# One transformer layer on one core: the first norm's rows loaded a second time by quadrants and turned by VectorE

## The chip, the cores and the metric

The kernel runs on one core of a Trainium2 chip. A core has TensorE (matrix products and the transposes that it makes as products with an identity, results in PSUM), VectorE, ScalarE and GpSimd (elementwise work; GpSimd cannot reach PSUM), SyncE, whose queue SP issues all DMA transfers here, and 16 DMA engines. The engines run their own lists of instructions and meet at semaphores. The metric is the time of one execution on the device in microseconds (us). Lower is better.

## The reference

Input is x, 2 x 2048 rows of 1024, f32. "Attention" is taken over the 32 heads of one row, not over rows:

```python
h = layernorm(x)                                   # (x - mean) / sqrt(var + 1e-5)
q, k, v = (h @ w.T + b for w, b in ...)            # each [row, 32 heads, 32]
scores = einsum('bshd,bstd->bsht', q, k) / sqrt(32)
x = x + einsum('bsht,bstd->bshd', softmax(scores), v)
h = layernorm(x)
gates = h @ gate_w.T                               # 8 experts, top 2, softmax over the two
x = x + h @ base_w.T + base_b + 2.0 * sum_e w_e * (h @ lora_A[e].T) @ lora_B[e].T
```

## The kernel before

**Tiles.** The 4096 rows are 32 tiles of 128 rows, one tile per step t. All weights stay in SBUF as f16 pairs, a high and a low part, and each f32 product is made of two or three f16 products. Step t makes tile t's projections (k, q, v; each in two halves of 512 columns, `project`, L1164 and L1173), its scores and its softmax, and for tile p = t - 1 the context product, the second norm, the experts and the base projection (`dense`, L1274). Steps 0, 1 and 31 are written out, steps 2 to 30 are a hardware loop on each compute engine; SP's list is unrolled. Step 0 and the first part of step 1 also prepare the weights (scales, splits into parts), so engines work there in another order.

**TensorE's order in a step:** k half 0, context of t - 1, k half 1, q half 0, q half 1, `turn2` (the second norm's transposes of tile t - 1), v half 0, v half 1, `experts`, attention scores (`attend`, L1227), then `dense_all`: 24 products for half 0, 6 for half 1, `turn1(t + 1)`, 9 more, `turn_low`, 9 more, `dense_lora`. `turn1` and `turn2` are eight f32 transposes of 128x128 each through `turn_rows` (L1235), into the PSUM tile `attn_ps` (called `rows_ps` in this layout).

**The first norm of tile t + 1**, done during step t:

- SP loads the rows into `ld` (L432, 128 pieces of 4 KB), once `centred` says that the tile before has left it.
- ScalarE, `centre`: sum of the row (L608), negated mean (L610), `xn = ld - mean` (L612), sum of squares (L614). It stands behind `x2_high` and ahead of b's high part (L686).
- GpSimd, `row_root`: three operations on one column (L478, L480, L482), rstd.
- ScalarE, `row1_scale`: `xn *= rstd` (L619).
- TensorE, `turn1`: transposes of `xn`.
- ScalarE, `x1_high` (L583), and VectorE, `x1_low` (L903): the transposed rows as f16 high and low parts, `x_hi` and `x_lo`, which the next step's projections read.

`xn` is used by the second norm as well (`norm2`, L847, by VectorE; then `turn2`, `x2_high` L591, `x2_low` L908).

**The rest of the chain to the scores of tile t.** VectorE adds the biases to k (L891), turns each row's heads (`turn_first`, L989); ScalarE takes k's high part (L677, semaphore `a_hi_ready`), VectorE its low part (`first_low`, L994); SP spreads both to a block diagonal (`spread_k`, L404, eight transfers). VectorE adds q's biases, makes `x2_low`, turns q (L1089); ScalarE takes q's high part (L686), GpSimd its low part (`second_lo`, L492, semaphore `b_lo_ready`). `attend` waits for `b_lo_ready` and for the spread k. VectorE then adds v's biases (two L891), and turns v when q's low part is made (L1097). After the scores follow the softmax (L1105, L1107, ScalarE's exp L698, L1113 to L1117), its transpose (L1123) and spreading of v's parts by ScalarE and VectorE (L342) for the context product.

**Semaphores.** Engines work their lists in order. A wait stops everything behind it on that engine.

Of the kernel before, what the change touches and what calls it, by code (L numbers as in the profile page):

```python
# [27 lines left out]
P = 128  # L28
QD = 32
NQ = P // QD  # L30
# [34 lines left out]
def block_kernel(nc, x, wT, agT, lora_b, biases, out):  # L65
    T = x.shape[0] // P
    with ExitStack() as ctx:
# [40 lines left out]
        rstd1 = columns[:, 16:17]  # L108
# [11 lines left out]
        w_chunk_sum = sb("w_chunk_sum", [P, NG, KC])  # L120
# [43 lines left out]
        xn = carve(HID)  # L164
        ev = carve(HID)
# [32 lines left out]
        squares = sb("squares", [P, HID], F16)  # L198
# [67 lines left out]
        centred = sem("centred")  # L266
# [4 lines left out]
        row1_ready = sem("row1_ready")  # L271
# [76 lines left out]
        flag_ps = low_ps[:, P:2 * P]  # L348

# [16 lines left out]
        def _(sp):  # L366
# [55 lines left out]
            def step(t, prev, nxt):  # L422
                if prev:

                    sp.wait_ge(x1_ready, t)
                    sp.dma_start(res, rows(x, t)).then_inc(res_loaded, 16)
                first_hi(t)
                first_lo(t)
                if t + 2 < T:

                    sp.wait_ge(centred, t + 1)
                    sp.dma_start(ld, rows(x, t + 2)).then_inc(ld_loaded, 16)  # L432
                if t == 1:

                    sp.wait_ge(w_lo_done["base"], KC)
                    sp.dma_start(lora_up[:, :], lora_b).then_inc(lora_loaded, 16)
                if prev and nxt:

                    sp.wait_ge(base_free, 2 * t + 2)
                    sp.dma_start(rows(out, t - 1), y).then_inc(y_stored, 16)  # L440
                elif not prev:

                    sp.wait_ge(w_lo_done["v"], KC)
                    sp.dma_start(res, rows(x, 0)).then_inc(res_loaded, 16)
# [18 lines left out]
        def _(pool):  # L463
# [11 lines left out]
            def row_root(t):  # L475
# [6 lines left out]
                nc.gpsimd.tensor_tensor(rstd1[:, :], root1[:, :], x_scale[:, :], ALU.mult).then_inc(rstd_ready1, 1)  # L482
# [30 lines left out]
            def step(t, prev, nxt):  # L513
                if prev:
                    root(t - 1, var_ready2, rstd_ready2)
                    base_bias(t - 1, x1)
                if nxt:
                    row_root(t + 1)
                if prev:
                    second_lo(t)  # L520
                v_low(t)
# [8 lines left out]
        def _(act):  # L530
# [49 lines left out]
            def x1_high(t):  # L580

                act.wait_ge(turned1, t + 1)
                nc.scalar.copy(x_hi[:, :, :], rows_ps).then_inc(xhi_ready, 1)  # L583
# [15 lines left out]
            def centre(t, prev):  # L599

                act.wait_ge(ld_loaded, 16 * (t + 1))
                if prev:

                    act.wait_ge(turned2, t - 1)
                else:

                    act.wait_ge(turned1, 1)
# [4 lines left out]
                nc.scalar.activation(xn, ld, ACT.Identity, bias=neg_mean[:, 0:1]).then_inc(centred, 1)  # L612
                act.wait_ge(centred, t)
                nc.scalar.activation(squares[:, :], xn, ACT.Square, accum_out=square_sum[:, :]).then_inc(squared, 1)  # L614

            def row1_scale(t):

                act.wait_ge(rstd_ready1, t)
                nc.scalar.activation(xn, xn, ACT.Copy, scale=rstd1[:, 0:1]).then_inc(row1_ready, 1)  # L619
# [11 lines left out]
            def first_step():  # L631
# [9 lines left out]
                centre(1, False)  # L641
                gate_sums()
                row1_scale(1)
# [6 lines left out]
                sums("base", 3, 5)  # L650

# [17 lines left out]
            def step(t, prev, nxt):  # L669
                if not prev:  # L670
                    return first_step()

# [6 lines left out]
                if nxt:  # L679
                    centre(t + 1, prev)  # L680
# [6 lines left out]
                if nxt:  # L687
                    row1_scale(t + 1)
# [36 lines left out]
        def _(dve):  # L725
# [173 lines left out]

            def x1_low(t):  # L900

                dve.wait_ge(xhi_ready, t + 1)
                nc.vector.tensor_tensor(x_lo[:, :, :], rows_ps, x_hi[:, :, :], ALU.subtract).then_inc(xlo_ready, 1)  # L903
# [7 lines left out]
            dve.wait_ge(consts_set, EXPERTS + 4)  # L911
# [69 lines left out]
            def norm2(p, rows_before, x1):  # L981

                dve.wait_ge(turned1, rows_before)
# [13 lines left out]
            def first_step():  # L997
# [43 lines left out]
                scale("ag")  # L1041
                x1_low(1)
# [26 lines left out]
            def step(t, prev, nxt):  # L1069
                if not prev:  # L1070
                    return first_step()
                if prev:
# [5 lines left out]
                    norm2(t - 1, t + 1, x1)  # L1078
# [13 lines left out]
                add_bias(t, 0, "v", 1, v_acc, v_biased)  # L1092
                add_bias(t, 1, "v", 2, v_acc, v_biased)
# [44 lines left out]
            def tail(t):  # L1138
# [3 lines left out]
                norm2(t - 1, t, x1_last)  # L1142
# [12 lines left out]
        def _(pe):  # L1155
# [41 lines left out]
            def spread_max(g):  # L1197

                pe.wait_ge(max_diags, SCALED.index(g) + 1)
                nc.tensor.matmul(late_max_ps if g in ("ag", "base") else max_ps, ones[:, :], max_diag, start=True,  # L1200
# [37 lines left out]
            def turn1(t):  # L1238

                pe.wait_ge(row1_ready, t)  # L1240
                pe.wait_ge(shifted, t)
                turn_rows(turned1)
# [57 lines left out]
            def dense_all(p):  # L1300
# [19 lines left out]
            def first_step():  # L1320
# [28 lines left out]
                turn1(1)  # L1349
# [4 lines left out]
            def step(t, prev, nxt):  # L1354
# [16 lines left out]
                project(SECOND, 0, 2, b_acc, any_low[0])  # L1371

# [72 lines left out]
```

## Time and profile before

| | |
|---|---|
| median of 3 runs (lowest, highest) | 1361.64 us (1360.42, 1361.67) |
| the profiled execution: time, span | 1360.58 us, 1358.4 us |
| mean granted TensorE clock | 0.987 |
| busy: TensorE, its weight loads | 1297.6 us (96%), 688.9 us (51%) |
| busy: VectorE, ScalarE, GpSimd | 1077.9 us (79%), 689.0 us (51%), 259.8 us (19%) |
| DMA | 33047 packets, 87.41 MB, 64 GB/s |

All durations come from the profiled execution. Its time is 2.2 us longer than its span, which goes from the first to the last instruction. A line of the profile names kernel line, engine, operation, tiles (`work` is one buffer that holds ld, xn, res, x1, y, turned and others; `columns` holds single columns such as mean and rstd) and count, and in brackets how long the engine had been idle before and what released it. PE is TensorE, PEld its weight loads, DVE VectorE, ACT ScalarE, POOL GpSimd.

### The profile page before, as it was taken

How to read it: one execution, taken by the hardware profiler on the slowest of the kernel's cores; microseconds unless marked ns; L12 is line 12 of the kernel's file. 1: busy time of each engine (PE TensorE's matmuls, PEld its weight loads, DVE VectorE, ACT ScalarE, POOL GpSimd, SP SyncE). 2: the span in 40 equal slices, each digit the busy share in tenths (PEclk: the TensorE clock that was granted, in tenths of full speed). 3: DMA queues.
4: the chain of work that ended last, by engine and by line, in shares of the span. 5: the costliest groups of instructions: out<-in, count | busy, mean ns of one | idle time of the engine just before them, and what ended most of it. 6: DMA issues, size and time to landing. Idle time of an engine off the chain costs nothing.

```text
span 1358.4 us, 29896 instructions
## 1 busy us (share of the span) xinstructions
PE 1297.6 (96%) x12446; PEld 688.9 (51%) x12446; DVE 1077.9 (79%) x1556; ACT 689.0 (51%) x987; POOL 259.8 (19%) x239
## 2 busy tenths in 40 slices
PE   4767999999999999999999999999999999999996
PEld 1443555555555555555555555555555555555553
DVE  5878887887788778877887887788778877887874
ACT  6774445544454555445445544454555445445531
POOL 0011121222112122221121222112122221121220
PEclk9988999999999999999999999999999999999998
DMA  9521111111111111111111112111111111111110
GB/s 368 206 78 38 64 57 46 46 62 62 62 49 45 60 46 46 62 62 62 41 52 46 46 62 62 62 50 45 59 47 47 62 62 62 40 52 46 31 48 31
DMA packets 33047, 87.41 MB, mean 64 GB/s; under 512 B 6656, under 2 KB 7680, under 8 KB 33024
## 3 DMA queue, kind: packets, MB, share of 16 engines
q1 hardware_dynamic: 33024, 87.10, 19.5%
q8 instruction: 15, 0.25, 0.1%
q14 instruction: 8, 0.07, 0.0%
HBM read 53.52 MB, written 16.78 MB: 52 GB/s over the span
## 4 chain that ended last, share of the span: by engine, by line
PE 89%; DVE 4%; ACT 3%; issue 2%; DMA 0%; SPq 0%; POOL 0%; DVEq 0%; ACTq 0%; POOLq 0%
PE acc L1164 23%; PE dense_acc L1274 23%; PE acc L1173 23%; PE attn_ps L1227 7%; PE attn_ps L1235 4%; PE dense_acc L1282 4%; PE low_ps L1257 1%; PE low_ps L1259 1%; PE low_ps L1258 1%; ACT work L342 1%; PE dense_acc L1297 1%; ACT base_parts L540 1%; DVE base_parts L798 1%; DVE v_parts L798 1%; ACT w_hi_q L564 0%
## 5 line engine op out<-in xcount | busy, mean ns | idle before, releaser
L1274 PE MATMUL dense_acc<-base_parts,x 128*128 128x512 f16 x1488 | 334.7, 379 | 0.0
L342 ACT COPY work<-work 32x512 f16<-32x512 f16 x384 | 236.0, 614 | 8.8
L1274 PEld LDWEIGHTS dense_acc<-base_parts,x 128*128 128x128 f16 x1488 | 143.1, 98 | 160.3
L891 DVE SCALAR_TENSOR_TENSOR work<-acc,acc_to_a,biases_sb 128x512 f32<-128x512 f32 x192 | 143.7, 750 | 83.4 <-PE acc L1173 77.8
L677 ACT CAST work<-work 128x1024 f16<-128x1024 f32 x31 | 32.4, 1046 | 338.6 <-DVE work L989 338.6
L487 POOL TENSOR_TENSOR columns<-columns 128x1 f32<-128x1 f32 x33 | 18.1, 549 | 647.1 <-DVE columns L841 647.1
L1164 PE MATMUL acc<-w_hi_q,x_hi 128*128 128x512 f16 x496 | 118.9, 383 | 5.9 <-DVE work L891 5.9
L1164 PE MATMUL acc<-w_hi_k,x_hi 128*128 128x512 f16 x496 | 120.5, 387 | 2.4 <-issue 2.4
L1173 PE MATMUL acc<-w_hi_q,x_lo 128*128 128x512 f16 x496 | 118.4, 382 | 0.0
L1173 PE MATMUL acc<-w_hi_k,x_lo 128*128 128x512 f16 x496 | 117.2, 379 | 0.0
L1164 PE MATMUL acc<-v_parts,x_hi 128*128 128x512 f16 x496 | 117.2, 379 | 0.0
L1173 PE MATMUL acc<-v_parts,x_lo 128*128 128x512 f16 x496 | 117.2, 379 | 0.0
L1227 PE MATMUL attn_ps<-work 128*32 128x128 f16 x6144 | 97.8, 220 | 8.7 <-ACT work L342 6.2
L1227 PEld LDWEIGHTS attn_ps<-work 128*32 128x32 f16 x6144 | 86.6, 97 | 26.0 <-issue 14.8
L498 POOL TENSOR_TENSOR work<-work 128x1024 f16<-128x1024 f32 x32 | 68.1, 2127 | 114.7 <-ACT work L693 109.4
L693 ACT CAST work<-work 128x1024 f16<-128x1024 f32 x31 | 32.4, 1045 | 104.0 <-DVE work L1097 104.0
L1164 PEld LDWEIGHTS acc<-w_hi_q,x_hi 128*128 128x128 f16 x496 | 48.8, 99 | 65.6 <-DVE work L891 6.4
L504 POOL TENSOR_TENSOR work<-work,biases_sb 128x1024 f32<-128x1024 f32 x32 | 75.6, 2362 | 32.0 <-DVE work L847 32.0
L1164 PEld LDWEIGHTS acc<-w_hi_k,x_hi 128*128 128x128 f16 x496 | 46.7, 99 | 68.9 <-issue 23.2
L968 DVE STREAM_TRANSPOSE work<-attn_ps 128x1024 f32<-128x1024 f32 x32 | 62.2, 1944 | 22.6 <-PE attn_ps L1227 22.6
L1235 PE MATMUL attn_ps<-ident,work 128*128 128x128 f32 x512 | 68.2, 277 | 11.8 <-DVE work L847 11.8
L1173 PEld LDWEIGHTS acc<-w_hi_q,x_lo 128*128 128x128 f16 x496 | 48.9, 99 | 59.7 <-issue 2.2
(184 smaller groups left out, 2065.1 us busy)
## 6 DMA issues: line engine op xcount, KB each, us to landing
work<-x_dram SPq DMA_DIRECT2D x64, 512.0 KB, 3.5
work<-work SPq DMA_DIRECT2D x256, 64.0 KB, 2.0
out_dram<-work SPq DMA_DIRECT2D x31, 512.0 KB, 2.9
work<-wT_dram SPq DMA_DIRECT2D x17, 512.0 KB, 5.6
v_parts<-wT_dram SPq DMA_DIRECT2D x8, 512.0 KB, 13.8
base_parts<-wT_dram SPq DMA_DIRECT2D x5, 512.0 KB, 10.8
biases_sb<-bias_dram SPq DMA_DIRECT2D x4, 512.0 KB, 7.5
base_parts<-agT_dram SPq DMA_DIRECT2D x1, 544.0 KB, 9.7
```

The source lines that it names most:

```text
L342: copy(diag[c * QD:(c + 1) * QD, :, c, j::NQ, :], src).then_inc(vdiag_ready, 1)
L498: nc.gpsimd.tensor_tensor(v_parts_t[:, :, 1, :], turned3, v_parts_t[:, :, 0, :], ALU.subtract).then_inc(v_lo_ready, 1)
L504: nc.gpsimd.tensor_tensor(x1, x1, bias["base"][:, :], ALU.add).then_inc(x1_biased, 1)
L677: nc.scalar.copy(k_parts[:, 0, :, :], turned3).then_inc(a_hi_ready, 1)
L891: nc.vector.scalar_tensor_tensor(out=ev[:, s], in0=acc[bank][:, :], scalar=acc_to_a[:, i:i + 1], in1=bias[g][:, s], op0=ALU.mult, op1=ALU. ...
L968: nc.vector.transpose(turned.rearrange("p (h d) -> p d h", h=HEADS), attn_ps[:, :].rearrange("p (t d) -> p d t", t=QD)).then_inc(ctx_turne ...
L1164: nc.tensor.matmul(dst, x_hi[:, k, :], w_hi[g][:, k, cols], start=(k == 0), stop=False)
L1173: mm = nc.tensor.matmul(dst, x_lo[:, k, :], w_hi[g][:, k, cols], start=False, stop=(k == KC - 1))
L1227: mm = nc.tensor.matmul(attn_ps[c * QD:(c + 1) * QD, i4 * P:(i4 + 1) * P], dense_parts[:, i, dense_part, :], diag[:, spread_part, :, i, :] ...
L1235: mm = nc.tensor.transpose(rows_ps[:, k, :], xn[:, k * P:(k + 1) * P], ident[:, :])
L1274: nc.tensor.matmul(dense_acc[n][:, :], rows_part[:, k, :], w_part[:, k, cols], start=(k == 0 and m == 0), stop=False)
L1282: nc.tensor.matmul(dense_acc[n][:, :], low[:, :], lora_up[:, n * HALF:(n + 1) * HALF], start=False, stop=True).then_inc(base_acc, 1)
```

## The change

The first norm of tiles 1 to 31 no longer passes through TensorE's transposes. (Tile 0 stays as it was.) VectorE's transpose turns each 32x32 block of a tile in place. So the rows are loaded a second time, in an order in which block-wise turning gives the whole transpose: partition 32b + t of the new layout holds, for each of 8 chunks k and 4 quadrants q, 32 elements of row 32q + t. Each piece of that load is 32 elements, 128 bytes, 1024 pieces for each of four transfers. Since a partition now holds four different rows, it needs their four means and rstds. They are carried by a product: `same_row` (128x128, one where two partitions have the same number within their quadrant) times `stat_rows` (each row's rstd and -mean * rstd, placed in the columns of its own quadrant).

```diff
 # SP
+            def load_quads(t):
+                sp.wait_ge(squared, t)
+                src = rows(x, t).rearrange("(q t) (k b c) -> b t k q c", q=NQ, b=NQ, c=QD)
+                for b in range(NQ):
+                    dst = ld[b * QD:(b + 1) * QD, :].rearrange("t (k q c) -> t k q c", k=KC, q=NQ)
+                    sp.dma_start(dst, src[b]).then_inc(quads_loaded, 16)
...
             def step(t, prev, nxt):
                 if prev:
+                    if nxt:
+                        load_quads(t + 1)
                     sp.wait_ge(x1_ready, t)
                     sp.dma_start(res, rows(x, t)).then_inc(res_loaded, 16)
                 first_hi(t)
                 first_lo(t)
+                if not prev:
+                    load_quads(1)
+                    sp.wait_ge(w_lo_done["v"], KC)
+                    sp.dma_start(res, rows(x, 0)).then_inc(res_loaded, 16)
                 if t + 2 < T:
-                    sp.wait_ge(centred, t + 1)
+                    sp.wait_ge(x1_turned_ready, t + 1)
                     sp.dma_start(ld, rows(x, t + 2)).then_inc(ld_loaded, 16)
 # GpSimd, row_root: behind rstd1; row_root(t + 1) now stands ahead of root(t - 1)
+                nc.gpsimd.tensor_tensor(neg_mean_rstd, rstd1, neg_mean[:, :], ALU.mult).then_inc(shift_ready1, 1)
+                pool.wait_ge(shift_ready1, t)
+                nc.gpsimd.tensor_tensor(stat_rows[:, :, :], row_stats[:, :].unsqueeze(2).to_broadcast([P, 2, NQ]),
+                                        in_quad[:, :].unsqueeze(1).to_broadcast([P, 2, NQ]),
+                                        ALU.mult).then_inc(stat_rows_ready, 1)
 # ScalarE
-            def centre(t, prev):  ...   # sum, mean, xn = ld - mean, sum of squares
-            def row1_scale(t):    ...   # xn *= rstd
+            def row_statistics(t):
+                act.wait_ge(ld_loaded, 16 * (t + 1))
+                act.wait_ge(xlo_ready, t)
+                ...                         # sum and negated mean as before
+                nc.scalar.activation(squares[:, :], ld, ACT.Square, bias=neg_mean[:, 0:1],
+                                     accum_out=square_sum[:, :]).then_inc(squared, 1)
+            def normalise_quads(t):
+                act.wait_ge(quad_spread, t)
+                nc.scalar.copy(quad_stats[:, :, :].rearrange("p s q -> p (s q)"), quad_ps).then_inc(quad_copied, 1)
+                act.wait_ge(quad_copied, t)
+                act.wait_ge(quads_loaded, 16 * NQ * t)
+                quads = ld.rearrange("p (k q c) -> p q k c", k=KC, q=NQ)
+                for q in range(NQ):
+                    nc.scalar.activation(quads[:, q, :, :], quads[:, q, :, :], ACT.Identity,
+                                         bias=quad_stats[:, 1, q:q + 1],
+                                         scale=quad_stats[:, 0, q:q + 1]).then_inc(quads_scaled, 1)
 # ScalarE's step: both at its head, ahead of k's high part
+                if nxt:
+                    row_statistics(t + 1)
+                    normalise_quads(t + 1)
                 act.wait_ge(at_ready, t + 1)
 # ScalarE's step 0: row_statistics(1) in centre's place; normalise_quads(1) ahead of exp
 # ScalarE, x1_high(t), t > 0: waits x1_turned_ready and scored, reads x1_turned in SBUF
 # VectorE, between the two v bias adds of a step; in step 0 behind scale("ag")
+            def turn_quads(t):
+                dve.wait_ge(quads_scaled, NQ * t)
+                dve.wait_ge(xlo_ready, t)
+                nc.vector.transpose(x1_flat[:, :], ld).then_inc(x1_turned_ready, 1)
 # VectorE, once, ahead of bias_bounds: selectors(), three small operations
 # TensorE
-            def turn1(t):  ...   # waits row1_ready and shifted, turn_rows(turned1)
+            def spread_stats(t):
+                pe.wait_ge(stat_rows_ready, t)
+                ...                         # t == 1: also max_all for "ag"
+                nc.tensor.matmul(quad_ps, same_row[:, :], stat_rows[:, :, :].rearrange("p s q -> p (s q)"), start=True,
+                                 stop=True).then_inc(quad_spread, 1)
 # TensorE's step
                 project(SECOND, 0, 2, b_acc, any_low[0])
+                if nxt:
+                    spread_stats(t + 1)
...
-                dense(1, 0, KC // 4)
-                turn1(p + 2)
-                dense(1, KC // 4, 5 * KC // 8)
+                dense(1, 0, 5 * KC // 8)
```

`quad_ps` is 8 columns of the PSUM tile `low_ps`. `squares`, where ScalarE drops the squares, now shares memory with `x1_turned`; `w_chunk_sum`, used in the weight preparation, shares memory with `xn`. VectorE's `norm2` waits for `turned2` of the tile before instead of `turned1`. The second load writes into `ld`, over the rows of the first load, and the four activations and the transpose work from there.

## Rows read from the trace of the kernel before

**Rows 1.** The page, chain that ended last, by line, shares of the span.

```profile
PE acc L1164 23%; PE dense_acc L1274 23%; PE acc L1173 23%; PE attn_ps L1227 7%; PE attn_ps L1235 4%; PE dense_acc L1282 4%; PE low_ps L1257 1%; PE low_ps L1259 1%; PE low_ps L1258 1%; ACT work L342 1%; PE dense_acc L1297 1%; ACT base_parts L540 1%; DVE base_parts L798 1%; DVE v_parts L798 1%; ACT w_hi_q L564 0%
```

**Rows 2.** Busy time of each engine in one step, us, instructions in brackets.

```profile
620.86:660.05 39.19, 39.19 (x383) 20.83 (x382) 31.80 (x45) 19.59 (x29) 8.05 (x7) 1.00 0.17 54
```

**Rows 3.** Timeline of TensorE, end of one step: start, duration, what.

```profile
614.27 1.04 PE L1235 MATMUL attn_ps<-ident,work 128*128 128x128 f32 x8
615.14 2.10 PE L1274 MATMUL dense_acc<-base_parts,x 128*128 128x512 f16 x9
617.09 0.27 PE L1265 MATMUL low_ps<-ident,low 128*128 128x128 f32 x1
617.20 2.11 PE L1274 MATMUL dense_acc<-base_parts,x 128*128 128x512 f16 x9
```

**Rows 4.** Timeline of TensorE in steps 0 and 1.

```profile
86.14 0.49 PE L1200 MATMUL low_ps<-base_parts,low 128*128 128x128 f32 x2 [1.83 <-DVE base_parts L756]
86.47 1.85 PE L1235 MATMUL attn_ps<-ident,work 128*128 128x128 f32 x8
...
118.22 3.59 PE L1164 MATMUL acc<-w_hi_q,x_hi 128*128 128x512 f16 x8 [5.92 <-DVE work L891]
```

**Rows 5.** Timeline of ScalarE in one step of the loop.

```profile
621.32 2.53 ACT L342 COPY work<-work 32x512 f16<-32x512 f16 x4
634.79 1.05 ACT L677 CAST work<-work 128x1024 f16<-128x1024 f32 x1 [10.94 <-DVE work L989]
...
638.21 1.06 ACT L608 ACTIVATE squares<-work 128x1024 f16<-128x1024 f32 x1
...
639.63 1.15 ACT L612 ACTIVATE work<-work,columns 128x1024 f32<-128x1024 f32 x1
...
641.87 1.03 ACT L686 CAST work<-work 128x1024 f16<-128x1024 f32 x1
...
656.59 0.27 ACT L629 COPY low<-low_ps 128x128 f32<-128x128 f32 x1 [1.04 <-PE low_ps L1265]
```

**Rows 6.** Timeline of VectorE in the same step.

```profile
635.87 1.23 DVE L994 TENSOR_TENSOR work<-work 128x1024 f16<-128x1024 f32 x1 [0.40 <-ACT work L677]
...
638.35 1.23 DVE L908 TENSOR_TENSOR x<-attn_ps,x 128x1024 f16<-128x1024 f32 x1 [0.59 <-ACT x L591]
...
644.21 0.75 DVE L891 SCALAR_TENSOR_TENSOR work<-acc,acc_to_a,biases_sb 128x512 f32<-128x512 f32 x1 [1.95 <-PE acc L1173]
...
655.19 1.25 DVE L1123 STREAM_TRANSPOSE work<-work 128x1024 f32<-128x1024 f32 x1
```

**Rows 7.** Timeline of GpSimd in the same step.

```profile
642.04 0.19 POOL L478 TENSOR_TENSOR columns<-columns 128x1 f32<-128x1 f32 x1 [6.81 <-ACT squares L614]
...
643.08 2.13 POOL L492 TENSOR_TENSOR work<-work 128x1024 f16<-128x1024 f32 x1
```

**Rows 8.** Timeline of TensorE in the same step, attention scores.

```profile
645.52 0.69 PE L1227 MATMUL attn_ps<-work 128*32 128x128 f16 x36
```

**Rows 9.** SP's timeline, 620 to 662; then DMA of 629 to 634, 40 slices.

```profile
629.48 0.33 SPq L426 DMA_DIRECT2D work<-x_dram  x1
635.87 4.95 SPq L404 DMA_DIRECT2D work<-work  x8
...
DMA  0000000000094495499979977100000000000000
...
work<-x_dram SPq DMA_DIRECT2D x1, 512.0 KB, 3.2
```

**Rows 10.** DMA of 3.6 to 3.9 us, then of 41.3 to 41.7 us.

```profile
DMA packets 247, 0.03 MB, mean 93 GB/s; under 512 B 242, under 2 KB 242, under 8 KB 247
...
q1 hardware_dynamic: 246, 0.13, 115.3%
```

**Rows 11.** Timeline of ScalarE in step 1.

```profile
114.58 1.15 ACT L564 ACTIVATE base_parts<-work,w_scale_bits 128x1024 f16<-128x1024 f32 x1
126.59 1.04 ACT L677 CAST work<-work 128x1024 f16<-128x1024 f32 x1 [10.86 <-DVE work L989]
```

More of the change, by code:

```diff
@@ L197, in block_kernel @@
         x_lo = sb("x_lo", [P, KC, P], F16)
-        squares = sb("squares", [P, HID], F16)
+        x1_flat = sb("x1_turned", [P, HID])
+        x1_turned = x1_flat[:, :].rearrange("p (k n) -> p k n", k=KC)
+        squares = x1_flat[:, 0:HID // 2].bitcast(F16)
+        same_row_small = xn[:, 0:QD]
+        same_row = sb("same_row", [P, P])
+        in_quad = sb("in_quad", [P, NQ])
+        row_stats = sb("row_stats", [P, 2])
+        rstd1 = row_stats[:, 0:1]
+        neg_mean_rstd = row_stats[:, 1:2]
+        stat_rows = sb("stat_rows", [P, 2, NQ])
+        quad_stats = sb("quad_stats", [P, 2, NQ])
         low = sb("low", [P, ER])
@@ L580, in x1_high @@
             def x1_high(t):
-                act.wait_ge(turned1, t + 1)
-                nc.scalar.copy(x_hi[:, :, :], rows_ps).then_inc(xhi_ready, 1)
+                if isinstance(t, int) and t == 0:
+                    act.wait_ge(turned1, 1)
+                    nc.scalar.copy(x_hi[:, :, :], rows_ps).then_inc(xhi_ready, 1)
+                else:
+                    act.wait_ge(x1_turned_ready, t)
+                    act.wait_ge(scored, t)
+                    nc.scalar.copy(x_hi[:, :, :], x1_turned).then_inc(xhi_ready, 1)
             def x2_high(p):
@@ L650, in first_step @@
                 sums("base", 3, 5)
+                normalise_quads(1)
                 act.wait_ge(shifted, 1)
@@ L910, in _ @@
             x1_low(0)
-            dve.wait_ge(consts_set, EXPERTS + 4)
+            selectors()
             bias_bounds()
@@ L979, in attention_end, with norm2 @@
                 ln_stats(p, 1, x1, mean_ready2, var_ready2)
-            def norm2(p, rows_before, x1):
-                dve.wait_ge(turned1, rows_before)
+            def norm2(p, x1):
+                if isinstance(p, int) and p == 0:
+                    dve.wait_ge(turned1, 1)
+                else:
+                    dve.wait_ge(turned2, p)
                 normalise(p, 1, x1, rstd_ready2, xn2_ready)
@@ L1041, in first_step @@
                 scale("ag")
+                turn_quads(1)
                 x1_low(1)
@@ L1092, in step @@
                 add_bias(t, 0, "v", 1, v_acc, v_biased)
+                if nxt:
+                    turn_quads(t + 1)
                 add_bias(t, 1, "v", 2, v_acc, v_biased)
@@ L1199, in spread_max @@
                 pe.wait_ge(max_diags, SCALED.index(g) + 1)
+                if g == "base":
+                    pe.wait_ge(quad_copied, 1)
                 nc.tensor.matmul(late_max_ps if g in ("ag", "base") else max_ps, ones[:, :], max_diag, start=True,
@@ L1348, in first_step @@
                 spread_max("ag")
-                turn1(1)
+                spread_stats(1)
                 pe.wait_ge(flag_ready, 1)
```

66 lines of the change are left out of this document (32 added, 34 removed).

## The prediction, made before the change was built or run

> **What bounds the kernel.** I read first the chain that ended last [rows 1]: TensorE's lines hold it, the three of the projections and of the base product with 23% each, and the rows' transposes of L1235, which the change halves, are 4%. Then the busy time of one stretch of 39.19 us, a step of the steady loop [rows 2]: TensorE is busy for all of it, VectorE for 31.8 us, ScalarE for 19.6, GpSimd for 8. So a step lasts as long as TensorE's instruction list, and every other engine matters only where TensorE would have to wait for it. Last the timeline of one step, for how close those places are. I take the step that TensorE begins at 620.86. The one place without room is the attention product at 645.52 [rows 8]: it needs the low part that GpSimd makes from 643.08 to 645.21 [rows 7], and that hangs on ScalarE's and VectorE's chain from 634.79 on [rows 5, 6].
>
> **TensorE, removed.** turn1, eight transposes: they start at 614.27 and the next matmul at 615.14 [rows 3], 0.87 us. 30 steps (1 to 30) have it: 26.1 us. The turn1 of the first step is costed with the start below.
>
> **TensorE, added.** spread_stats, one f32 product of 128x128 by 128x8 per step, between two projections. No row has it. From above: the f32 product of 128x128 by 128x128 (two passes, as the x2 says) starts at 86.14 and the next instruction at 86.47 [rows 4], 0.33 us. From below: the one-pass f32 transpose of L1265, 0.11 us from start to the next start [rows 3]. With 8 columns the streaming shrinks, but two f32 weight loads and the load behind them have nothing to hide under; I take 0.30. In 29 steps (the one in step 1 lies in the start) 8.7 us.
>
> **Waits that go with it.** In the step at 620.86, ScalarE ends its spreading at 623.85 [rows 5] and would start row_statistics. Before, statistics with the centring took from 638.21 to 641.87; without L612 (1.15) and with 0.09 more for a bias operand (1.15 against 1.06) that is 2.6 us: squared at 626.5. GpSimd's three small operations took from 642.04 to 643.08, where the next began [rows 7]; with two more at some 0.3 each, stat_rows stands at 628.3. TensorE ends its third projection at 632.77, so it doesn't wait (4.4 us of room), and the product is done at 633.1. ScalarE stands at normalise_quads from 626.5 to then; behind it on its queue is the high part of k, which before waited 10.94 us for VectorE's transpose until 634.79 [rows 5]. So this wait is in idle time.
>
> **ScalarE.** It loses centring and scaling (1.15 each) and gains a copy of 8 columns (under 0.27, as L629) and four activations of 256 elements. From 128 elements in 0.27 and 1024 in 1.06 [rows 5], 256 take 0.38; with 0.09 for the second operand and partly overlapped I take 0.5, four are 2.1 us (bounds 1.6 and 2.6, the latter four of the 512-element copies). If the second load has landed, they run from 633.4 to 635.5, and k's high part comes 0.7 us later than before.
>
> **Can the chain carry 0.7 us?** VectorE's first_low moves from 635.87 to 636.6, its next bias add ends at 638.5; x2_low before began at 638.35 after 0.59 us idle [rows 6] and now waits for TensorE's turn2, 0.3 later by the product: 638.65. The transpose behind it ends at 641.8. There ScalarE was busy with statistics until 641.87 and GpSimd with the root chain until 643.08; both are gone from there, so b's low part starts at about 642.9, not 643.08, and ends at 645.0. TensorE comes at 645.8 (645.52 plus 0.3). That leaves 0.75 us, and with the 0.15 at x2_low k's high part may start as late as 636.4, which means: loads landed by 634.3. The k spreading on SP (issued from 635.87 to 640.82 [rows 9]) had 4.7 us from its last issue to 645.52, more than the 3.2 a whole row load takes to land, and keeps about that.
>
> **VectorE.** turn_quads adds one contiguous 128x1024 transpose, 1.25 us as L1123, between two v bias adds; the second of them stood 1.95 us idle for TensorE at 644.21 [rows 6]. Hidden. Were it as long as the strided transposes (some 2 us), it would be late by 0.1. x1_high and x1_low no longer wait for TensorE and read the same count of elements: nothing. The three selector operations lie once in the start, before a wait for the weights: nothing, at most 1 us.
>
> **SP and the load by quadrants.** This is the term that decides. Four transfers of 1024 pieces of 128 bytes, 4096 packets where a row load has 128. SP has nothing between the y store of the step before and the load of res at 629.48 [rows 9], which is now queued behind the four and needed only in the next step. Issue at 626.55. A row load's data began 0.9 us behind its issue and landed 0.45 after its last packet [rows 9]. For the rate, two bounds: 242 packets of 32 bytes in 0.3 us, and 246 packets of 544 bytes in 0.4 us [rows 10]. 4096 at these rates are 5.1 and 6.7 us; 128 bytes lie nearer 32, I take 5.5. Landed: 633.4 (bounds 633.0 and 634.6). The need is 633.4 and the limit 634.3: hidden, with under 1 us to spare, and at the upper bound 0.3 us of stall a step.
>
> **The start, once.** In step 0, turn1 ran from 86.47 to 88.32 behind spread_max [rows 4], exp before it on ScalarE, x1_high and all the spreading right behind it. Now the product stands there; VectorE must have read spread_max first, so I put it at 87.0 to 87.35; then copy, four activations (to 89.8), exp, which waits behind them on ScalarE (to 91.0), and x1_high at 91.2: 2.9 us later, and ScalarE's chain carries that to the base weights. In step 1, ScalarE comes to row_statistics only when its part of the base weights is done, at 115.73 [rows 11] plus 2.9: squared at 121.3, product at 123.1 to 123.4, where TensorE before went on at 118.22 [rows 4]; load landed at 128.2 (121.3 + 0.05 + 0.9 + 5.5 + 0.45), k's high part at 130.4, before 126.59 [rows 11]: 3.8 us later. One chain gives 5.2, the other 3.8, and TensorE and the low part meet at the attention product. I take 4.8 (bounds 2 and 9).
>
> **Sum.** -26.1 + 8.7 + 4.8 = -12.6 us against 1360.58, the profiled execution's own time (span 1358.4, 2.2 around it): 1348.0. That execution is 1.1 below the median of the three runs, 1361.64; from the median it is 1349.0, which I give. A measurement of this kernel tells some 0.2%, 2.7 us, from no change.
>
> **Rivals.** (1) The load is a little late. In the 0.4 us of 544-byte packets the records take 115% of 16 engines [rows 10]: 7.4 us of engine time for 246 packets, 30 ns each. If 128-byte packets cost as much and nothing overlaps, 256 per engine are 7.7 us, landing 635.6, stall 1.3 x 30 = 39 us: 1388. Every value between is possible; it decides from a landing at 634.3 on, and it turns slower when the stall passes 0.42 us, a landing at 634.7. For it: the limit is 0.9 us from my value. Against: both rates of rows 10 land it before 634.7. (2) Writes under a certain size cost a second access: each packet then occupies its engine twice. At twice my bounds, 10.2 to 13.4 us, the load lands at 639.7 in the middle, 5.4 us late, 162 us in all: 1511. Against: in rows 10 the 32-byte packets go through faster than 544-byte ones and not slower. (3) No gain: the product costs what the transposes did, because TensorE waits for GpSimd's chain of five, or drains. Against it are the 4.4 us of room; it would give 1361 to 1366. (4) The other engines become the bound by ScalarE: at 0.75 us for each quadrant activation k's high part is at 636.5 and the stall 0.1, so it needs the load late as well; about 1350 to 1365.
>
> The Trainium skill, "DMA: Bandwidth & Descriptors", Specifications, gives 512 bytes as the smallest transfer for line rate and says that below it the engine does a read-modify-write; that is rival 2, and the rule speaks against this change. Rows 10 don't bear out a doubling at 32 bytes, but no row shows 128-byte writes into SBUF. By the rule the sum would be rival 2's, by the rows mine.
>
> **Chances.** Forecast, load hidden, 1342 to 1356: 0.56. Rival 1: 0.22, a third of it not slower. Rival 2: 0.10. Rival 3: 0.05. Rival 4: 0.07, 0.02 of it faster. Faster by over 0.2%: 0.56, 0.03 from rival 1 and 0.02 from rival 4, 0.61. Within 0.2%: 0.04 from rival 1, 0.03 from rival 3, 0.01 from rival 4, 0.08. Slower: 0.15 + 0.10 + 0.02 + 0.04 = 0.31. The range runs from 1342 (product 0.15, start 2: -26.1 + 4.4 + 2 = -19.7 from 1361.64) to 1390, just above rival 1's price; it leaves out rival 2 and the ends. The likeliest case alone: 1342 to 1356 (product 0.33, start 9, and 0.03 us of stall a step at the other end: -26.1 + 9.6 + 9 + 1 = -6.5).
>
> **What the profile after would show.** L1235 at eight per step, not sixteen; the small product at 0.3 us; a step of 38.6 us; ScalarE's wait before the four activations put down to TensorE (right) or to the load (rivals 1 and 2); the load's landing 6.9 us behind its first issue; TensorE idle before the attention product, by GpSimd's low part, in every step, if I am wrong. Steps above 39.19 us would mean the load.

## The result, and the profile after

| | before | after |
|---|---|---|
| median of 4 runs (lowest, highest) | 1361.22 us (1360.42, 1361.67) | 1341.24 us (1338.74, 1342.09) |
| ratio, with its 95% interval | | 0.9852 (0.9836 to 0.9867) |
| the profiled execution: time, span | 1360.58, 1358.4 us | 1342.09, 1339.8 us |

The kernel became 20.0 us faster, 1.5%. The forecast was 1349.0 with a range from 1342 to 1390. The direction is right. The time lies 0.8 us below the range.

The chain that ended last, by line, has L1309 (the transposes of rows) at 2%, where it was 4% [rows 1]:

```profile
PE acc L1235 24%; PE acc L1244 24%; PE dense_acc L1351 23%; PE attn_ps L1301 7%; PE dense_acc L1359 4%; PE attn_ps L1309 2%; PE low_ps L1334 1%; PE low_ps L1336 1%; PE low_ps L1335 1%; ACT work L357 1%; PE dense_acc L1374 1%; ACT base_parts L575 1%; DVE v_parts L842 1%; DVE base_parts L842 1%; ACT w_hi_q L599 0%
```

Busy time by engine over one step, which TensorE begins at 612.05, to be held against [rows 2]:

```profile
612.05:650.51 38.46, 38.46 (x376) 20.17 (x375) 32.97 (x46) 19.77 (x32) 8.51 (x9) 1.00 0.27 68
```

The step takes 38.46 us, not 39.19. TensorE is still busy for all of it, so nothing has taken its place as the bound. VectorE has gained 1.17 us and still has 5.5 us free.

The same step on TensorE, around the new product, at the attention product and at the place where turn1 stood [rows 3, 8]:

```profile
623.98 0.28 PE L1318 MATMUL low_ps<-stat_rows,same_row 128*128 128x8 f32 x2
624.12 1.89 PE L1235 MATMUL acc<-w_hi_q,x_hi 128*128 128x512 f16 x8
...
636.86 1.52 PE L1301 MATMUL attn_ps<-work 128*32 128x128 f16 x96
...
646.74 0.27 PE L1342 MATMUL low_ps<-ident,low 128*128 128x128 f32 x1
646.85 2.11 PE L1351 MATMUL dense_acc<-base_parts,x 128*128 128x512 f16 x9
```

The product follows the projection without idle time and the next projection starts 0.14 us behind it. The duration column says 0.28 because it reaches into the next instruction; start to start is what it costs. The attention product at 636.86 has no wait in brackets.

ScalarE's new chain in the step, ahead of k's high part [rows 5]:

```profile
624.30 0.17 ACT L656 COPY quad_stats<-low_ps 128x8 f32<-128x8 f32 x1 [6.57 <-PE low_ps L1318]
624.58 2.08 ACT L662 ACTIVATE work<-work,quad_stats 128x256 f32<-128x256 f32 x4
626.56 1.03 ACT L725 CAST work<-work 128x1024 f16<-128x1024 f32 x1
```

ScalarE waited 6.57 us for the product, in what was idle time before. The four activations took 2.08 us from first start to the end (2.1 was taken) and waited for no load. VectorE, with the new transpose at 633.48 [rows 6]:

```profile
633.48 1.23 DVE L960 STREAM_TRANSPOSE x_turned<-work 128x1024 f32<-128x1024 f32 x1
...
635.55 0.75 DVE L935 SCALAR_TENSOR_TENSOR work<-acc,acc_to_a,biases_sb 128x512 f32<-128x512 f32 x1 [0.84 <-PE acc L1244]
```

The idle time of 1.95 us ahead of the last v bias add is 0.84 now; the transpose stands in it. On GpSimd, `stat_rows` is done at 619.44, 4.5 us before TensorE asks for it, and q's low part is done at 636.06, 0.8 us ahead of the attention product [rows 7]:

```profile
633.93 2.13 POOL L527 TENSOR_TENSOR work<-work 128x1024 f16<-128x1024 f32 x1 [7.47 <-ACT work L732]
```

SP issues the four quadrant transfers and then `res`:

```profile
617.75 3.19 SPq L422 DMA_DIRECT2D work<-x_dram  x4
621.00 0.67 SPq L452 DMA_DIRECT2D work<-x_dram  x1
```

DMA packets of the microsecond from 621 to 622, then the queue's share of 16 engines:

```profile
DMA packets 1439, 0.18 MB, mean 181 GB/s; under 512 B 1439, under 2 KB 1439, under 8 KB 1439
...
q1 hardware_dynamic: 1439, 0.18, 116.2%
```

In this microsecond 1439 packets of 128 bytes went through. 116.2% of 16 engines for 1 us over 1439 is 12.9 ns for a packet, and one left each 0.7 ns. The rates taken from [rows 10] were 1.2 and 1.6 ns a packet (0.3 us over 242, 0.4 us over 246). At this rate 1024 pieces take 0.7 us, and SP took 0.8 us to issue them. In the microsecond before, from 620 to 621, only 792 packets went at 63.4%, so there the engines stood partly idle. The fourth transfer was issued at 619.9. The view of the microsecond from 620 gives the time from its issue to its landing:

```profile
work<-x_dram SPq DMA_DIRECT2D x1, 128.0 KB, 4.0
```

So the load was there at 623.9, 6.1 us behind its first issue and 0.7 us ahead of the first activation.

**Start.** TensorE in steps 0 to 2, after; then the same attention product and the same begin of step 2, before:

```profile
85.52 0.36 PE L1318 MATMUL low_ps<-stat_rows,same_row 128*128 128x8 f32 x2 [0.47 <-DVE w_max L804]
...
120.92 0.59 PE L1318 MATMUL low_ps<-stat_rows,same_row 128*128 128x8 f32 x2 [9.44 <-POOL stat_rows L515]
...
136.92 1.52 PE L1301 MATMUL attn_ps<-work 128*32 128x128 f16 x96
...
150.58 1.89 PE L1235 MATMUL acc<-w_hi_k,x_hi 128*128 128x512 f16 x8
```

```profile
136.01 1.52 PE L1227 MATMUL attn_ps<-work 128*32 128x128 f16 x96 [1.89 <-POOL work L492]
...
150.53 1.89 PE L1164 MATMUL acc<-w_hi_k,x_hi 128*128 128x512 f16 x8
```

The attention product of step 1 comes 0.9 us later than before, where the forecast had 4.8. The 0.9 compares one execution with one. The execution after was already 0.4 us ahead at the attention product of step 0 (78.94 against 79.32), and such differences come between executions too: in experiments 1 to 4 that product began between 78.24 and 79.08. Counted from it, the start costs 1.3 us. Step 2 begins at 150.58 against 150.53; turn1's 0.87 us of this step is in that. ScalarE, and SP's issue of the load, in the same stretch:

```profile
89.50 1.04 ACT L625 CAST x_hi<-x_turned 128x1024 f16<-128x1024 f32 x1 [0.27 <-DVE x_turned L960]
...
115.45 1.15 ACT L599 ACTIVATE base_parts<-work,w_scale_bits 128x1024 f16<-128x1024 f32 x1
...
125.50 2.08 ACT L662 ACTIVATE work<-work,quad_stats 128x256 f32<-128x256 f32 x4 [3.79 <-DMA work<-x_dram]
```

```profile
119.17 2.77 SPq L422 DMA_DIRECT2D work<-x_dram  x4
```

**End.** The last step's attention product came 21.3 us earlier, at 1290.48 instead of 1311.81. From there to the end, busy time and clock, before and then after:

```profile
1311.81:1358.40 46.59, 32.68 (x332) 16.29 (x330) 24.55 (x50) 12.36 (x20) 5.03 (x3) 0.93 0.06 24
```

```profile
1290.48:1339.80 49.32, 35.70 (x332) 18.11 (x330) 24.62 (x50) 12.37 (x20) 5.03 (x3) 0.85 0.06 22
```

This stretch has no part in the change and the same number of instructions on every engine, and it took 2.7 us longer. In the last context product TensorE's granted clock was 0.50 after (1.2 GHz) and 1.00 before (2.4 GHz); TensorE's rows of it, before and after:

```profile
1326.49 1.52 PE L1227 MATMUL attn_ps<-work 128*32 128x128 f16 x96 [2.69 <-ACT work L342]
```

```profile
1305.01 2.75 PE L1301 MATMUL attn_ps<-work 128*32 128x128 f16 x96 [2.54 <-ACT work L357]
```

So the span shrank by 18.6 us and not by 21.3. This differs from run to run: the four spans of the changed kernel were 1336.5 to 1339.8. Over the eleven traces of this case the same stretch took 46.6 to 49.3 us, and that of before is the shortest of all: in each of the other ten the last context product took longer than 1.52 us, 2.07 to 2.75. In experiment 8, the kernel before with one small edit, it took 2.23 and the stretch 47.7. So the length of this stretch goes with the execution and not with the change.

### The profile page after: what moved, and what is told of

It reads as the page before. It is cut to its first block, busy times and chain, and to the rows that moved or that the text cites. A ratio compares the mean times of both kernels' runs of the same rounds, so it can differ in the third digit from the quotient of the medians.

```text
span 1339.8 us, 29902 instructions
## 1 busy us (share of the span) xinstructions
PE 1276.6 (95%) x12260; PEld 669.7 (50%) x12260; DVE 1113.1 (83%) x1590; ACT 694.4 (52%) x1080; POOL 274.0 (20%) x301
## 4 chain that ended last, share of the span: by engine, by line
PE 90%; DVE 4%; ACT 3%; issue 2%; DMA 0%; SPq 0%; POOL 0%; DVEq 0%; ACTq 0%; POOLq 0%
PE acc L1235 24%; PE acc L1244 24%; PE dense_acc L1351 23%; PE attn_ps L1301 7%; PE dense_acc L1359 4%; PE attn_ps L1309 2%; PE low_ps L1334 1%; PE low_ps L1336 1%; PE low_ps L1335 1%; ACT work L357 1%; PE dense_acc L1374 1%; ACT base_parts L575 1%; DVE v_parts L842 1%; DVE base_parts L842 1%; ACT w_hi_q L599 0%
## 5 line engine op out<-in xcount | busy, mean ns | idle before, releaser
L1351 PE MATMUL dense_acc<-base_parts,x 128*128 128x512 f16 x1488 | 329.8, 379 | 0.0
L527 POOL TENSOR_TENSOR work<-work 128x1024 f16<-128x1024 f32 x31 | 66.0, 2130 | 231.0 <-ACT work L732 231.0
L656 ACT COPY quad_stats<-low_ps 128x8 f32<-128x8 f32 x31 | 5.2, 166 | 195.7 <-PE low_ps L1318 195.7
L505 POOL TENSOR_TENSOR columns<-columns 128x1 f32<-128x1 f32 x31 | 5.9, 191 | 459.6 <-ACT x_turned L650 452.8
L533 POOL TENSOR_TENSOR work<-work 128x1024 f16<-128x1024 f32 x32 | 68.1, 2128 | 116.7 <-ACT work L737 114.6
```

Of the source, the lines that this page charges most:

```text
L527: nc.gpsimd.tensor_tensor(dense_parts[:, :, 1, :], turned3, dense_parts[:, :, 0, :], ALU.subtract).then_inc(b_lo_ready, 1)
L533: nc.gpsimd.tensor_tensor(v_parts_t[:, :, 1, :], turned3, v_parts_t[:, :, 0, :], ALU.subtract).then_inc(v_lo_ready, 1)
L1351: nc.tensor.matmul(dense_acc[n][:, :], rows_part[:, k, :], w_part[:, k, cols], start=(k == 0 and m == 0), stop=False)
```

## The experiments

The ratio is always to the kernel before, run beside it on the same chip. "After" is the changed kernel.

**1. The transposes back in.** Eight transposes at turn1's old place, in steps 1 to 30, whose result nobody reads. VectorE's second norm waits for them again, as it did in the kernel before.

```diff
-                dense(1, 0, 5 * KC // 8)
+                dense(1, 0, KC // 4)
+                pe.wait_ge(shifted, p + 2)
+                turn_rows(turned1)
+                dense(1, KC // 4, 5 * KC // 8)
```

> The changed kernel with TensorE's eight transposes of xn put back at their old place in steps 1 to 30; nothing uses their result. Theory A, the gain is TensorE's shorter list: a step goes from 38.46 us to 39.33 (plus 0.87), 30 x 0.87 = 26 us slower than the changed kernel, about 1367, so some 5 us above the kernel before. Theory B, the gain came from ScalarE's and VectorE's shorter path to x_hi and x_lo and not from the transposes: the step stays near 38.5 and the time within 5 us of 1341.

Measured 1368.25 us, 1.0057 (1.0040 to 1.0074), steps of 39.33 us. TensorE at that place:

```profile
616.25 1.04 PE L1309 MATMUL attn_ps<-ident,work 128*128 128x128 f32 x8
617.12 2.11 PE L1351 MATMUL dense_acc<-base_parts,x 128*128 128x512 f16 x9
```

From start to start 0.87 us, and the step is 0.87 longer. In the whole it is 27.0 us, of which 30 x 0.87 are 26.1: the removed term is the time of the transposes in TensorE's list.

**2. The product twice,** the same small product once more behind the first.

> The changed kernel with the small product (128x128 by 128x8, f32) issued twice each time. Theory A, the product costs the 0.14 us that lie between its start and the next start: a step of 38.60 us, 31 x 0.14 = 4 us slower than the changed kernel. Theory B, of the forecast, 0.30 us because two f32 weight loads stand bare, and the first one hides part of its price behind the projection in front of it: a step of 38.76, 9 us slower.

Measured 1346.56 us, 0.9894 (0.9878 to 0.9911), a step of 38.68 us. TensorE:

```profile
588.55 0.28 PE L1318 MATMUL low_ps<-stat_rows,same_row 128*128 128x8 f32 x2
588.69 0.37 PE L1320 MATMUL low_ps<-stat_rows,same_row 128*128 128x8 f32 x2
588.91 1.89 PE L1235 MATMUL acc<-w_hi_q,x_hi 128*128 128x512 f16 x8
```

The first costs 0.14 us, the second 0.22. The cost is between the two theories: a repeated product is dearer than the one in place, but by 0.08 us only. That the first one's weight load runs beside the last matmul of the projection is the likely reason; it isn't shown.

**3. The load issued behind `res`.** The call of `load_quads` stands behind `res` on SP.

```diff
-                    if nxt:
-                        load_quads(t + 1)
                     sp.wait_ge(x1_ready, t)
                     sp.dma_start(res, rows(x, t)).then_inc(res_loaded, 16)
+                    if nxt:
+                        load_quads(t + 1)
```

> The changed kernel with the load by quadrants issued behind the load of res instead of ahead of it: its first issue moves from 617.75 to about 621.1 in the step shown, 3.3 us later. The last 128-byte packets ran until about 622.9 and ScalarE's activations began at 624.58, so the load had some 1.3 us to spare. Theory A, the load is one bound that is not reached, and behind it the chain to the attention product has 0.8 us: ScalarE waits for the load, k's high part is 2 us late, TensorE stalls 1.0 to 1.4 us a step, 30 to 42 us slower than the changed kernel. Theory B, there is a lot more room in that chain than I think: under 10 us slower.

Measured 1418.15 us, 1.0426 (1.0408 to 1.0443). The steps are no longer equal, 40.45 to 42.31 us with a mean of 40.94; the one shown took 40.81. In it `res` was issued at 614.28; SP's next row, then ScalarE, then TensorE:

```profile
614.66 3.70 SPq L422 DMA_DIRECT2D work<-x_dram  x4
```

```profile
621.45 2.08 ACT L661 ACTIVATE work<-work,quad_stats 128x256 f32<-128x256 f32 x4 [3.40 <-DMA work<-x_dram]
```

```profile
632.80 1.52 PE L1300 MATMUL attn_ps<-work 128*32 128x128 f16 x96 [2.28 <-POOL work L526]
```

The activations now wait 3.40 us for the load and start 15.81 us behind the step's begin, 3.28 later than in after (12.53). TensorE waits 2.28 us for GpSimd's low part ahead of the attention product, and the step is 2.35 longer. 3.28 less 2.35 is 0.93 us: the room in the chain that the prediction worked out as 0.9. The size of the loss was 77 us and not the 30 to 42 expected, because the load was later than assumed. Its first issue came 3.32 us later in the step than in after (9.02 against 5.70 behind the step's begin). It took 6.79 us from there to use, where in after it had landed in 6.1, and the room before the first activation was 0.7 and not the 1.3 that was expected. 3.3 later and 0.7 longer, less the room of 0.7, are the 3.3 us by which the activations came late.

**4. The quadrants' transpose twice** on VectorE.

> The changed kernel with VectorE's transpose of the quadrants made twice (1.25 us more in each step). Theory A, it stands beside TensorE: the bias add behind it waited 0.84 us, so 0.4 us get through to VectorE's chain, which has 2 us before TensorE needs x_lo: within 1 us of the changed kernel, step 38.46. Theory B, VectorE at 83% is as good as full: each 1.25 us shows at least in part, 10 to 37 us slower.

Measured 1341.64 us, 0.9859 (0.9842 to 0.9875), a step of 38.46. VectorE, the second of the two transposes and what follows:

```profile
636.47 1.25 DVE L963 STREAM_TRANSPOSE x_turned<-work 128x1024 f32<-128x1024 f32 x1
637.64 0.71 DVE L936 SCALAR_TENSOR_TENSOR work<-acc,acc_to_a,biases_sb 128x512 f32<-128x512 f32 x1
```

The idle time ahead of the last bias add is used up and nothing else moves. VectorE's added work is hidden, with over a microsecond to spare.

**5. Late, but in whole rows.** As experiment 3, with each of the four transfers as 32 whole rows of 4 KB. The rows arrive in another order, so the norm is applied to other elements.

```diff
-                src = rows(x, t).rearrange("(q t) (k b c) -> b t k q c", q=NQ, b=NQ, c=QD)
+                src = rows(x, t).rearrange("(b t) n -> b t n", b=NQ)
...
-                    dst = ld[b * QD:(b + 1) * QD, :].rearrange("t (k q c) -> t k q c", k=KC, q=NQ)
+                    dst = ld[b * QD:(b + 1) * QD, :]
```

> The kernel e3_load_late, but the four transfers of the second load take whole rows: 32 packets of 4 KB each in place of 1024 pieces of 128 bytes. Every step still runs, on rows in another order, so the output is not the reference's. In e3 the activations could start 6.8 us after the load's first issue. Theory A, the pieces' size is what takes the time: SP issues four transfers in some 2 us, a whole row load lands 3.2 us after its issue, so the load is there about 5 us after its first issue, at most 0.9 us later than ScalarE could use it, which is the room: 1341 to 1350. Theory B, four transfers in place of one and the place behind res cost it: it stays near e3's 1418.

Measured 1376.33 us, 1.0111 (1.0094 to 1.0128), steps of 39.3 to 39.8 us with a mean of 39.55. SP issued the four from 600.77 on, in 1.82 us; ScalarE:

```profile
606.40 2.08 ACT L661 ACTIVATE work<-work,quad_stats 128x256 f32<-128x256 f32 x4 [2.23 <-DMA work<-x_dram]
```

The load still is late: 5.63 us from first issue to use, where about 5 was expected. Neither theory was met. Of the 77 us that experiment 3 lost against after, the late place alone costs 35 (1376.33 less 1341.24), and the small pieces add 42 in that place; by the mean step it is 1.1 and 1.4 us.

**6. A wide product.** A second product of the same weights with 112 columns instead of 8, into unused columns.

> The changed kernel with a second product of the same weights by 112 columns behind the small one (result unused). The second product of 8 columns in e2_product_twice added 0.22 us to a step. Theory A, a small f32 product costs its two weight loads and hardly its columns, 112 columns stream for 112 x 4 / 2.4 GHz = 0.19 us in all, of which the gap of the weight loads hides a part: 0.25 to 0.35 us more than the changed kernel per step, 8 to 11 us. Theory B, the columns come on top in full: 0.41 us per step, 13 us.

Measured 1350.92 us, 0.9920 (0.9903 to 0.9936), a step of 38.75 us: 0.29 more than in after, as theory A had it. TensorE, the second product and the projection behind it:

```profile
591.30 0.45 PE L1320 MATMUL low_ps<-ident,same_row 128*128 128x112 f32 x2
591.59 1.89 PE L1235 MATMUL acc<-w_hi_q,x_hi 128*128 128x512 f16 x8
```

0.29 us for 112 columns, against 0.22 for 8 in experiment 2. 104 columns more add 0.07 us, so most of such a product's time does not depend on its columns.

**7. The start in another order.** In step 0, ScalarE takes exp ahead of the activations, and the gate's high part behind them.

> The changed kernel with ScalarE's step 0 in another order: exp ahead of normalise_quads(1), where ScalarE stood idle for 3.06 us, and the high part of the gate weights (1.20 us) in the 1.3 us in which x1_high waits for VectorE's transpose. Theory A, the start hangs on ScalarE's chain to the base weights: k's high part of step 2's base work and all behind it come 0.8 us earlier; the time falls by 0.8 us, less than the timing can tell, the trace shows it at the attention product of step 1 (136.92 in the changed kernel). Theory B, it hangs on TensorE's 9.4 us wait for stat_rows in step 1: nothing moves.

Measured 1340.73 us, 0.9852 (0.9835 to 0.9868): no difference to after. ScalarE's base weights are done 0.4 us earlier, but in step 1 the activations start when they did:

```profile
125.49 2.08 ACT L662 ACTIVATE work<-work,quad_stats 128x256 f32<-128x256 f32 x4 [4.17 <-DMA work<-x_dram]
```

They wait 4.17 us for the second load instead of 3.79: it was issued 0.4 us earlier too (118.78 against 119.17), but it took 6.71 us to use and not 6.33. So the load's landing sets the start of this chain. TensorE came to the attention product of step 1 earlier than in after, and waited for GpSimd's low part:

```profile
136.85 1.52 PE L1301 MATMUL attn_ps<-work 128*32 128x128 f16 x96 [1.63 <-POOL work L527]
```

The product starts at 136.85 all the same, against 136.92 in after. The 0.8 us expected did not come.

**8. The kernel before, with its scaling of the rows later in step 0.** It is aimed at VectorE's L756, which stands ahead of TensorE's first product there [rows 4].

```diff
-                row1_scale(1)
                 sums("base", 0, 3)
+                row1_scale(1)
```

> The kernel before, with one edit: row1_scale(1) behind the three magnitude sums of base in step 0, so that ScalarE does not stand 5.13 us for GpSimd's rstd. In the kernel before, VectorE's L756 at 84.60 took 1.49 us beside GpSimd's v low part (83.88 to 86.00), in the changed kernel the same operation took 0.29 us with GpSimd at rest. Theory A, the start of the changed kernel was cheaper than forecast because the earlier sums take GpSimd's v low part out of VectorE's way: here too that operation takes 0.29 us and turn1 of step 0 starts about 1.2 us earlier than 86.47. Theory B, the 1.49 us had another reason: it stays.

One run, 1360.38 us. VectorE's operation, and the begin of step 2:

```profile
85.61 0.29 DVE L756 TENSOR_SCALAR base_parts<-ident,w_part_max 128x128 f32<-128x128 f32 x1
```

```profile
149.22 1.89 PE L1164 MATMUL acc<-w_hi_k,x_hi 128*128 128x512 f16 x8
```

L756 took 0.29 us instead of 1.49, once GpSimd's low part (80.80 to 82.93 here) no longer ran beside it. But it began 1.0 us later than before, because two products ahead of it on TensorE took longer (at 79.27, 2.19 us for 1.52, and at 81.39, 2.87 for 1.96), and turn1 started only 0.2 us earlier and not the 1.2 expected:

```profile
86.28 1.04 PE L1235 MATMUL attn_ps<-ident,work 128*128 128x128 f32 x8
```

Turn1 itself took 1.04 us and not 1.85. Step 2 began 1.3 us earlier, which is thus not the 1.2 of L756 alone. The total is within the runs of before all the same: the last attention product came 1.3 us earlier (1310.49), and the stretch behind it took 1.1 longer.

**9. Whole rows in place.** Experiment 5's transfers at the changed kernel's own place in the queue; the rows again arrive in another order.

> The changed kernel with the second load taking whole rows (4 KB packets, rows in another order, so the output is not the reference's) at the load's own place, ahead of res. In e5 the activations could start 5.6 us after the first issue, in e3 6.8 us; here both are ready before ScalarE comes. Theory A, the 128-byte pieces cost nothing as long as the load is hidden: a step of 38.46 us and 1341 us, within 2 us; only the wait in step 1 (3.79 us before L662) gets shorter, by 1 to 2 us. Theory B, 4096 packets a step slow the other transfers or the engines' memory traffic: 38.3 or less per step, over 4 us faster than the changed kernel.

Measured 1341.21 us, 0.9853 (0.9837 to 0.9869), a step of 38.46. In step 1, where the load is waited for, SP issued the four from 120.22 on, in 1.72 us; ScalarE:

```profile
124.38 2.08 ACT L662 ACTIVATE work<-work,quad_stats 128x256 f32<-128x256 f32 x4 [1.62 <-DMA work<-x_dram]
```

The load is used 4.16 us behind its first issue, not 6.33, and the total doesn't change: theory A. The small pieces cost 2.2 us of landing and none of the kernel's time. In step 1, the one step in which the load is waited for, the time gained was not usable: k's high part then waited 2.06 us for VectorE's transpose of k.

## Why the prediction came out as it did

**Right.** The mechanism: the step is TensorE's list, the transposes of turn1 leave it and all that replaces them, but for the small product, is hidden. The removed 0.87 us a step was confirmed by experiment 1, the 0.9 us of room for a late load by experiment 3, the four activations (2.08 us for 2.1) by the trace, VectorE's cover by experiment 4 and GpSimd's margin (4.5 us for 4.4) by the trace.

**Wrong: the product's term, +8.7.** The prediction said that "two f32 weight loads and the load behind them have nothing to hide under" and took 0.30 us, near the upper bound. It costs 0.14, near the lower, and experiments 2 and 6 show 0.22 for one more of its kind and 0.29 for one with 112 columns. Over 29 steps 0.14 is 4.1 us, 4.6 less.

**Wrong: the start's term, +4.8.** It was 0.9. Two steps of the working failed. The first put the product of step 0 at 87.0 ("VectorE must have read spread_max first, so I put it at 87.0 to 87.35"). It came at 85.52. In the kernel before VectorE's product with the identity, at 84.60, took 1.49 us beside GpSimd's low part, the first two rows below; in after it comes at 84.22 and takes 0.29, the last:

```profile
84.60 1.49 DVE L756 TENSOR_SCALAR base_parts<-ident,w_part_max 128x128 f32<-128x128 f32 x1
```

```profile
83.88 2.12 POOL L498 TENSOR_TENSOR work<-work 128x1024 f16<-128x1024 f32 x1 [5.32 <-ACT work L649]
```

```profile
84.22 0.29 DVE L800 TENSOR_SCALAR base_parts<-ident,w_part_max 128x128 f32<-128x128 f32 x1
```

Experiment 8 shows the same fall of this operation in the kernel before. It accounts for 1.2 us of the 1.5; the rest is within the 0.4 us by which this execution was ahead in any case. `x1_high` began at 89.50, 1.2 us later than before and not 2.9, and the base weights ended 0.9 later. The row of `x1_high` in the kernel before:

```profile
88.35 1.01 ACT L583 CAST x_hi<-attn_ps 128x1024 f16<-128x1024 f32 x1 [1.42 <-PE attn_ps L1235]
```

The second failed step is in step 1: the prediction took TensorE's late restart (5.2 us) as if all of it were lost. TensorE waited 9.44 us for the statistics and took up the projections 3.1 us late (121.36 against 118.22), but before it had waited 1.89 us at the attention product, for GpSimd's low part, and that wait is gone. On the other chain the load's first issue came at 119.17, 2.2 us earlier than forecast, and the load was 0.5 faster; k's high part came at 127.48, 0.9 behind that of before [rows 11], and GpSimd's low part ended at 136.71:

```profile
134.58 2.13 POOL L527 TENSOR_TENSOR work<-work 128x1024 f16<-128x1024 f32 x1 [6.63 <-ACT work L732]
```

The attention product followed at 136.92 without a wait, so TensorE and the low part met within 0.2 us. In experiment 7 TensorE stood 1.6 us for the low part and the product began within 0.1 us of the same time, so the low part's chain by itself gives the 0.9.

**Sum again, with what was measured.** -26.1 + 4.1 + 0.9 = -21.1, and the last attention product is indeed 21.3 us earlier. At the end 2.7 came back in the profiled execution; the median gained 20.0 in all. -12.6 had been forecast: 4.6 of the difference is the product, 3.9 the start, and the other way 1.1 is what the median shows less than this sum.

**The range.** Its lower end, 1342, took 0.15 for the product and 2 for the start. The product was 0.3 us below that over the steps and the start 1.1; with the median of before now 0.4 lower this would be 1340.1 (1361.22 less 21.1). The measured median is 1.1 above that, 1341.24; only one execution of each kernel was profiled, so that the end took this 1.1 in the median is likely and not shown. The step that failed in the range is the start's lower bound: 2 us, where the start cost 0.9 (1.3 counted from the attention product of step 0).

**The rivals.** The load was used 6.33 us behind its first issue in step 1, where it was waited for, and landed 6.1 behind it in the steady loop (6.9 was taken), so rival 1 didn't come about; experiment 3 shows what it would have cost had the load stood 3.3 us later. That the sum of this term came so near is partly luck. The prediction added 0.9 us to the first packet, 5.5 for the packets and 0.45 behind them; the packets of the load shown ran from 619.2 to 622.9, so the parts were 1.4, 3.7 and 1.0. The packets were faster than both bounds and the time around them was longer than taken. Rival 2, the doubled access: 12.9 ns for a 128-byte packet is less than the 30 ns of a 544-byte one, and nothing is 5 us late. The Trainium skill, "DMA: Bandwidth & Descriptors", Specifications, calls 512 bytes the smallest size for line rate; the trace agrees as far as 128 bytes in 12.9 ns are 9.9 GB/s an engine against 18 for 544 bytes in 30 ns. It gives no time for the read-modify-write that it names below this size; the doubled time that rival 2 took is not what the runs show. Rivals 3 and 4: TensorE lost 0.14 us and not 0.87, and ScalarE was never waited for in the steady loop.

**Open.** Why TensorE drops to 1.2 GHz in the last step of one execution and not of another was not tried. Nor was why the whole rows of experiment 5 took 5.6 us behind `res`. In the step shown there each of the four landed 3.7 to 4.2 us behind its own issue, with `res` (512 KB) issued 0.4 us ahead of them; in a step of experiment 9, with `res` behind them, it was 2.4 to 2.8. That the two loads shared the DMA engines fits this; no run separates it.

## What to carry to other kernels

Where one engine is busy for the whole step, moving its work to any engine with idle time is worth the start-to-start time of what leaves it, less that of what must stay. Price the small operation that stays by start-to-start rows of its kind and put both ends in the range, and before a wait in the start-up is given its price, see what the same engine waited for further on: what is already waited for there is not paid twice. A slow load costs nothing until it is late, and then every step pays. Here its place in the queue decided whether it was late: in its own place the small pieces cost nothing, behind `res` they cost 42 us on top of 35.

## What the runs showed of the hardware

- A f32 product of 128x128 weights by 8 columns between f16 projections took 0.14 us from start to start, the same once more behind it 0.22, and with 112 columns 0.29.
- Four DMA transfers of 1024 pieces of 128 bytes: SP's issue took 0.7 to 0.9 us each on average (2.77 to 3.70 for four), against 0.43 to 0.46 with 32 pieces of 4 KB; the packets took 12.9 ns each in the microsecond measured. The load was used 6.33 us behind its first issue in step 1, with whole rows 4.16.
- A VectorE operation on 128x128 f32 took 1.49 us when it began beside a GpSimd operation of 2.12 us on 128x1024 elements, and 0.29 without it. It ended at 86.09, 0.1 us behind GpSimd's (86.00). Two smaller VectorE operations on 128x1 and 128x2 elements, during the same GpSimd operation, took 0.16 and 0.15 us.
- At the end of the program the same 96 matmuls took 1.52 us in one execution and 2.75 in another, with the same idle time ahead of them to 0.15 us (2.69 and 2.54); over eleven traces they took 1.52 to 2.75.
